# Attention with three softmaxes per head: two heads' global keys as one 128-column weight tile, value products issued in pairs of key rows, ten probability buffers

## What is computed

```python
attn = q @ k.T * scale                      # 16 heads of 8 channels
local_out  = softmax(where(|i - j| <= 128, attn, -inf)) @ v
topk_out   = softmax(q @ k[top 128 rows].T * scale) @ v[top 128 rows]
global_out = softmax(q @ k[first 64 rows].T * scale) @ v[first 64 rows]
out = (local_out + topk_out + global_out) / 3
```

## Time and profile before

| | us |
|---|---|
| median of 3 runs | 555.68 (554.42 to 555.85) |
| profiled execution | 551.48, span 549.6 |
| granted TensorE clock, mean | 0.993 |
| PE busy | 491.7 (89%) |
| DVE busy | 390.3 (71%) |
| ACT busy | 355.1 (65%) |
| POOL busy | 311.8 (57%) |

### The profile page before, as it was taken

The page is one execution under the profiler, slowest core; times in us unless marked ns, Lnnn a source line. Parts: engine busy times, 40 slices in busy tenths (PEclk is TensorE's granted clock), DMA queues, the critical chain, the costliest instruction groups (busy, mean ns, idle before and its releaser), DMA issues.

```text
span 549.6 us, 13411 instructions
## 1 busy us (share of the span) xinstructions
PE 491.7 (89%) x4427; PEld 305.4 (56%) x4427; DVE 390.3 (71%) x1400; ACT 355.1 (65%) x835; POOL 311.8 (57%) x464
## 2 busy tenths in 40 slices
PE   6999899889768899899789998999998999889996
PEld 3577677667334355345355454545554553577874
DVE  4877876469986698898877789677797893145325
ACT  7588565788008666657656857766665657657753
POOL 3411065457599975655059976689708336354540
PEclk9999999999889999999999999999999999999999
DMA  7999011765300000000000000001000101775606
GB/s 217 350 337 306 8 44 49 248 213 185 89 7 15 4 14 14 5 13 14 11 8 12 11 8 13 14 28 29 20 13 4 36 25 57 245 232 172 202 15 192
DMA packets 46006, 47.81 MB, mean 87 GB/s; under 512 B 8788, under 2 KB 37594, under 8 KB 45937
## 3 DMA queue, kind: packets, MB, share of 16 engines
q1 hardware_dynamic: 42928, 41.37, 24.3%
q0 software_dynamic: 3008, 5.58, 3.2%
HBM read 11.32 MB, written 19.48 MB: 56 GB/s over the span
## 4 chain that ended last, share of the span: by engine, by line
PE 63%; DVE 19%; issue 8%; ACT 6%; DMA 2%; POOL 1%; SPq 0%; DVEq 0%; ACTq 0%; POOLq 0%
PE BANK L1912 6%; PE BANK L1809 6%; PE BANK L1857 4%; PE BANK L1999 4%; PE BANK L1887 4%; PE BANK L1765 3%; PE BANK L1915 3%; PE BANK L1777 3%; PE BANK L1918 3%; DVE SW L1392 2%; DVE M L1390 2%; DVE QST L1438 2%; PE BANK L1792 2%; PE BANK L1882 2%; PE BANK L1862 2%
## 5 line engine op out<-in xcount | busy, mean ns | idle before, releaser
L1090 ACT ACTIVATE PT<-BANK 128x256 f32<-128x256 f32 (+2 forms) x352 | 161.9, 487 | 98.1 <-PE BANK L1887 71.2
L698 POOL TENSOR_SCALAR OH<-IOTA,POS 128x128 bf16<-128x128 bf16 x240 | 140.4, 605 | 4.7 <-DVE OH L1553 3.4
L1433 DVE CUSTOM_DVE_ANT_0 XN_a<-BANK,BANDQ 128x256 f32<-128x256 f32 (+1 forms) x128 | 62.3, 487 | 29.4 <-PE BANK L1857 25.6
L1433 DVE CUSTOM_DVE_ANT_0 XN_c<-BANK,BANDQ 128x384 f32<-128x384 f32 (+1 forms) x128 | 62.4, 487 | 14.2 <-PE BANK L1857 13.1
L706 POOL TENSOR_TENSOR SUM<-NRM 128x128 f32<-128x128 f32 x16 | 7.3, 456 | 96.8 <-DVE NRM L1454 96.8
L1912 PE MATMUL BANK<-PT,V 128*32 128x256 f32 (+1 forms) x512 | 47.7, 444 | 9.0 <-ACT OS L1099 8.6
L1438 DVE TENSOR_REDUCE QST<-BANK 128x4 f16<-128x512 f32 x64 | 42.3, 690 | 9.9 <-PE BANK L1862 9.6
L730 POOL DMA_INDIRECT yt_late<-QKV,IDY_late x31 | 30.4, 980 | 27.4 <-DVE QKV L1311 22.7
L1809 PE MATMUL BANK<-XNT_ALL,W 128*128 128x512 f32 x96 | 45.3, 597 | 0.0
L907 ACT ACTIVATE PT<-BANK 128x512 f32<-128x512 f32 x48 | 27.8, 598 | 19.1 <-PE BANK L1809 18.8
L1882 PE MATMUL BANK<-BANDK,IDB 128*128 128x256 bf16 x128 | 35.2, 275 | 0.4 <-ACT PT L1090 0.3
(11 more groups left out here) (371 smaller groups left out, 1299.6 us busy)
## 6 DMA issues: line engine op xcount, KB each, us to landing
xs_late<-W SPq DMA_DIRECT2D x1, 6984.0 KB, 39.3
xs_early<-W SPq DMA_DIRECT2D x1, 4680.0 KB, 18.9
KZB<-W SPq DMA_DIRECT2D x16, 256.0 KB, 2.6
KZC<-W SPq DMA_DIRECT2D x15, 256.0 KB, 2.3
PT<-W SPq DMA_DIRECT2D x11, 256.0 KB, 2.4
QKV<-xs_late SPq DMA_DIRECT2D x31, 72.0 KB, 1.9
W<-w SPq DMA_DIRECT2D x2, 1024.0 KB, 8.8
QKV<-xs_early SPq DMA_DIRECT2D x23, 72.0 KB, 2.5
```

The costliest lines, as they stand in the source:

```text
L698: last = nc.gpsimd.tensor_scalar(OH[g % 2][:, i, t, :], IOTA[:, :], POS[:, t, c:c + 1], None, ALU.is_equal)
L1090: nc.scalar.activation(PT[u % PT_RING][:, 0:w], P2_BANK[u % SCORE_RING][:, 0:w], ACT.Exp, scale=SCALE).then_inc(S["exp_done"], 1)
L1433: nc.vector.tensor_tensor_reduce(out=JUNK[v % 2][:, 0:n], in0=P1_BANK[v % SCORE_RING][:, 0:n], in1=BANDQ[:, off:off + n], scale=1.0, scala ...
```

## The change

1. Global keys. The second head's 64 global keys go into the first head's key tile, beside that head's own: columns 512 to 639 of the even tile hold two heads, in different partitions, and the top keys move to columns 640 to 767 in all tiles. The global p2 is one matmul with a 128-column weight tile instead of two of 64 columns; the global p1 is four matmuls of 128 columns instead of eight of 64, and the order in the bank changes accordingly, which the maximum reads in another order. `spread` issues six DMAs per group instead of four.
2. Value products. Rows 0 and 1 are issued together at u = 9, rows 2 and 3 at u = 17, rows T and T + 1 at u = 1 of the next group.
3. `PT` has ten buffers instead of eight.

```diff
--- before.py
+++ after.py
@@ -37,6 +37,8 @@
 SCALE = float(1.0 / (DH ** 0.5))
 KW = L + N_GLOBAL + K_TOP
 KG0, KS0 = L, L + N_GLOBAL
+PAIR_KEYS, TOP_KEYS = slice(L, L + 2 * N_GLOBAL), slice(L + 2 * N_GLOBAL, L + 2 * N_GLOBAL + K_TOP)
+SPREADS = HG + HG // 2
 TAKEN = -3.0e38
 OFF = -1.0e30
 SHIFT = 24
@@ -51,7 +53,8 @@
 ROWS = T + 2
 LEAD = 8
 FIRST_LEAD = 4
-PT_RING = 8
+PT_RING = 10
+PV_AT = {9: (0, 1), 17: (2, 3)}
 SCORE_RING = 3
 PART = DH + 1
 NG = B * GROUPS
@@ -434,6 +437,10 @@
 
         def spread_done(g):
 
+            return 16 * SPREADS * (g // 2 + 1)
+
+        def top_spread_done(g):
+
             return 16 * HG * (g // 2 + 1)
 
         def full(*use):
@@ -527,10 +534,20 @@
                              ).then_inc(R[w.tag]["zeroed"], 16)
 
 
-            def spread(g, lo, hi, done):
+            def spread(g):
+
+                for i in range(HG):
+                    r, a = slice(32 * i, 32 * i + 32), i % 2
+                    last = L if a else KS0
+                    sp.dma_start(KZ[g % 3][i][r, 0:last], KALL[g % 2][r, 0:last]).then_inc(KEYS_IN[g % 2], 16)
+                    if a:
+                        sp.dma_start(KZ[g % 3][i - 1][r, KG0 + N_GLOBAL:KG0 + 2 * N_GLOBAL], KALL[g % 2][r, KG0:KS0]
+                                     ).then_inc(KEYS_IN[g % 2], 16)
+
+            def spread_top(g):
                 for i in range(HG):
                     r = slice(32 * i, 32 * i + 32)
-                    sp.dma_start(KZ[g % 3][i][r, lo:hi], KALL[g % 2][r, lo:hi]).then_inc(done, 16)
+                    sp.dma_start(KZ[g % 3][i][r, TOP_KEYS], KALL[g % 2][r, KS0:KW]).then_inc(TOP_KEYS_IN[g % 2], 16)
 
             def tile_numbers(w, n):
 
@@ -576,18 +593,18 @@
             sp.wait_ge(S["misc_free"], free("qk", 0) + 1)
 
             sp.wait_ge(S["heads_zero"], 3)
-            spread(0, 0, KS0, KEYS_IN[0])
+            spread(0)
             results(EARLY)
             sp.wait_ge(S["misc_free"], free("qk", 1) + 1)
-            spread(1, 0, KS0, KEYS_IN[1])
+            spread(1)
             for g in range(NG):
 
 
                 if g >= 2:
                     sp.wait_ge(S["misc_free"], free("qk", g) + 1)
-                    spread(g, 0, KS0, KEYS_IN[g % 2])
+                    spread(g)
                 sp.wait_ge(S["misc_free"], free("kv", g) + 1)
-                spread(g, KS0, KW, TOP_KEYS_IN[g % 2])
+                spread_top(g)
 
             sp.wait_ge(R["late"]["table"], 1)
             sp.wait_ge(R["late"]["scattered"], 16 * 2 * LATE.jt)
@@ -1411,7 +1428,7 @@
                 dve.wait_ge(S["misc_full"], full("kv", g))
                 if g >= 2:
 
-                    dve.wait_ge(TOP_KEYS_IN[g % 2], spread_done(g - 2))
+                    dve.wait_ge(TOP_KEYS_IN[g % 2], top_spread_done(g - 2))
                 nc.vector.tensor_scalar(KALL[g % 2][:, KS0:KW], MISC[:, 0:K_TOP], KSH[:, TOP:TOP + 1], None, ALU.add)
                 nc.vector.reduce_sum(VSEL[g % 3][:, :, PART:PART + DH],
                                      MISC[:, K_TOP:K_TOP + HG * 3 * DH].rearrange("p (i s d) -> p i d s", i=HG, s=3),
@@ -1439,7 +1456,7 @@
                                          AX_X).then_inc(S["max_done"], 1)
                 else:
                     nc.vector.reduce_max(qst[:, :, h:h + GPAIR, SHIFT + GLOBAL],
-                                         P1_BANK[v % SCORE_RING][:, :].rearrange("p (a t s) -> p t a s", a=GPAIR, t=T),
+                                         P1_BANK[v % SCORE_RING][:, :].rearrange("p (t a s) -> p t a s", a=GPAIR, t=T),
                                          AX_X).then_inc(S["max_done"], 1)
 
             def divide(g):
@@ -1857,15 +1874,13 @@
                     last = mm(bank[:, 0:(hi - lo) * P], q[:, t * P:(t + 1) * P], k[:, lo * P:hi * P], start=True, stop=True)
                 elif t == T:
                     if w == TOP_W:
-                        pe.wait_ge(TOP_KEYS_IN[g % 2], spread_done(g))
+                        pe.wait_ge(TOP_KEYS_IN[g % 2], top_spread_done(g))
                     for s in range(T):
-                        last = mm(bank[:, s * K_TOP:(s + 1) * K_TOP], q[:, s * P:(s + 1) * P], k[:, KS0:KW], start=True, stop=True)
+                        last = mm(bank[:, s * K_TOP:(s + 1) * K_TOP], q[:, s * P:(s + 1) * P], k[:, TOP_KEYS], start=True, stop=True)
                 else:
                     for s in range(T):
-                        for a in range(GPAIR):
-                            lo = (a * T + s) * N_GLOBAL
-                            last = mm(bank[:, lo:lo + N_GLOBAL], q[:, s * P:(s + 1) * P], KZ[g % 3][i + a][:, KG0:KS0],
-                                      start=True, stop=True)
+                        last = mm(bank[:, s * GPAIR * N_GLOBAL:(s + 1) * GPAIR * N_GLOBAL], q[:, s * P:(s + 1) * P], k[:, PAIR_KEYS],
+                                  start=True, stop=True)
                 last.then_inc(S["p1_done"], 1)
 
             def p2(g, r, n):
@@ -1887,11 +1902,9 @@
                     last = mm(bank[:, 0:(hi - lo) * P], KZ[g % 3][n][:, r * P:(r + 1) * P], QT2[g % 2][:, lo * P:hi * P],
                               start=False, stop=True, skip_group_check=True)
                 elif r == T:
-                    last = mm(bank[:, :], KZ[g % 3][n][:, KS0:KW], QT2[g % 2][:, :], start=True, stop=True)
+                    last = mm(bank[:, :], KZ[g % 3][n][:, TOP_KEYS], QT2[g % 2][:, :], start=True, stop=True)
                 else:
-                    for a in range(2):
-                        last = mm(bank[64 * a:64 * a + 64, :], KZ[g % 3][2 * n + a][:, KG0:KS0], QT2[g % 2][:, :],
-                                  start=True, stop=True)
+                    last = mm(bank[:, :], KZ[g % 3][GPAIR * n][:, PAIR_KEYS], QT2[g % 2][:, :], start=True, stop=True)
                 last.then_inc(S["p2_done"], 1)
 
             def pv(g, r):
@@ -2068,9 +2081,10 @@
                     p2(g, r, n)
                     for v in scored_beside(g, u):
                         p1(*divmod(v, UNITS_Q))
-                    if n == 1 and r:
-                        pv(g, r - 1)
-                    elif n == 1 and g:
+                    for row in PV_AT.get(u, ()):
+                        pv(g, row)
+                    if u == 1 and g:
+                        pv(g - 1, T)
                         pv(g - 1, T + 1)
                     if u == qk_at(g) and g + 2 < NG:
                         transpose_qk(g + 2)
...
+            pv(NG - 1, T)
             pv(NG - 1, T + 1)
```

## The result

The changed kernel takes 566.48 us (median of 4 runs, 565.38 to 567.12), the kernel before in the same comparison 555.05. The ratio is 1.0226, with a 95% interval of 1.0197 to 1.0254: slower, by 10.9 to 14.1 us of 555. The forecast was 566.5.

A forecast was written before the change was run, and what follows sets the result against it. PE sets the pace, with ACT or DVE right behind in every stretch but A. Group sums of 12.7 us, taken as 11, on the profiled 551.48 give 562.5; 4.2 to the median makes 566.5, own range 560 to 572, overall 546 to 574.

The forecast's parts named there:

- A: Group 10 from unit 0 to unit 2: 2.15 us plus the top row's product, 0.98, gives 3.1 us.
- B: Group 10, unit 2 to the value product's end at u = 9: stays 5.6 us, ACT's queue still setting it.
- C: Group 10, from there to unit 18: 6.96 to 7.7 us, row 2's product, 0.78, no longer under DVE's work.
- D: Group 10, unit 18 to the next unit 0: 3.19 to 2.6 us, PE waiting nearly 1 us for QT2.
- The sum over the groups: All groups: +1.2 us for each of groups 7 to 13, 8.4 together; with the rest 12.7, of which 11 taken.
- a pair's own saving: On PE, a value product directly following another saves 0.12 us, three times a group: 0.36 us.
- the projection, 0.65 us, takes the place of the row 0 product under ACT's queue: Early groups, projection at u = 6: about -0.6 us in B, leaving +0.4 a group, 1.6 for groups 1 to 4.
- The cut from 12.7 to 11: Whole kernel: 11 of 12.7 us taken, since a walk counts every wait and treats B and C as independent.
- What costs nothing: SP's two extra copies a group (1.2 us) and the ten buffers add no wait; the buffers belong to the pairs.
- That PE alone counts: Rival, all 16 groups: PE's 0.8 us a group is gained, -13 us, 543; needs D below 2.2, C below 7; chance 0.22.
- The cancelling rival: Rival: gains and waits cancel, 555.7 within 2 us; needs a C loss of about 0.4, not 0.8; chance 0.13.
- The largest one: Rival: waits add up further, groups 1 to 6 also lose 1.2 us each, +17 us, 573; chance 0.13.

The follow-up runs named there:

- e8_row0_at7: Changed kernel with no value products paired, row 0's product at u = 7, the others in their old places, ten buffers: 553.30 us, ratio 0.9999.
- e9_tile_os_first: e1_tile with ACT's copy of the output bank behind exponential 2, ahead of the key copies, instead of behind exponential 3: ratio 0.9914, on another chip.
- e7_pair01: Changed kernel with only rows 0 and 1 still paired, the other value products in their old places: 551.96 us, ratio 0.9969.
- e5_row2_early: Changed kernel with row 2's product back at u = 13, the other pairs kept: 561.29 us, ratio 1.0161.
- e6_again19: Changed kernel with the second query transpose at u = 19 instead of 20: 563.85 us, ratio 1.0202.
- e2_pairs: Kernel before with the new order of value products and ten buffers, without the new global key tile: 566.08 us, ratio 1.0228.
- e3_ring8: Changed kernel with eight probability buffers instead of ten: 578.10 us, ratio 1.0450.
- e1_tile: Changed kernel with the old order of value products and eight buffers, so only the new global key tile: 551.39 us, ratio 0.9943.

## Why the prediction was right

**What bounds the kernel.** Right in that each stretch is set by the engine that was named for it, and that the new waits are larger than what PE saves: in group 10 PE's idle time went from 1.06 to 2.07 us. One sign did not come: PE's busy time was to fall by 13 us and fell by 3.1. The traces do not say how much of the rest is the lower clock (0.983 for 0.993) and how much the way through the array that the last matmul ahead of each new wait shows as busy. What PE saves is read from the distances between starts, below.

**A, forecast 3.1 us.** 3.01. The second of two products starts 0.88 us behind the first (376.19 to 377.07), not 0.98 as in the last group before.

**B, forecast 5.6, "not gained, only named differently".** 5.42, against 5.51 before by instruction starts. The tile alone, with the old order, has 5.49. `e8_row0_at7` and `e9_tile_os_first` put the product or the copy in two other orders and have 5.47 and 5.41, and `e7_pair01`, with this pair alone, has 5.42. What it is below the forecast is the pair again: 640 columns take 1.21 us where the step had 1.3 to 1.4.

**C, forecast 7.7.** 7.58. DVE's first top maximum starts 1.19 us behind the start of C, and the step in the shared bank 5.45 us behind it, forecast 1.17 and 5.41. Row 2's product is owed behind it. Only the place of the wait was told wrong: not p1's of units 14 to 16 wait in this group, but the gathering ahead of them, for DVE's division. Over the run p1's wait for top maxima 5.2 us, 4.6 before. `e5_row2_early` brings C back to 6.94.

**D, forecast 2.6.** 2.54, set by QT2: `e6_again19` makes it 2.05, and `e2_pairs` has the same 2.54 with 0.45 us more of work. The Trainium skill's page "TensorEngine Tiling (Array Packing)", section "PSUM Bottleneck", says that tiling speeds up TensorE but not the emptying of PSUM. The trace agrees: ACT, which empties the banks, is busy for 2.48 of D's 2.54 us.

**The sum over the groups** is where it was right by luck. That the median met the forecast to 0.02 us says little: the walk was to give 562.5 us for the profiled execution, and that took 566.20. The traces are 14.8 us apart for the forecast's 11, and the 3.8 missing were made up by the distance from the profiled execution to the median, taken as 4.2 us and 0.3 in the changed kernel.

Now the 14.8 us, group by group. An ordinary group was forecast at +1.2 and group 10 measured +0.74 by instruction starts (17.81 to 18.55); groups 7 to 13 came to 5.2 us instead of 8.4. What was mis-sized is a pair's own saving, 0.12 us each in the sum and some 0.25 measured: a lone product of rows 0 and 1 cost 0.10 + 0.57 and 0.10 + 0.78, 1.55, and the pair 0.10 + 1.21. Three pairs a group make about 0.4 us.

The other side was too low. The step that failed is "the projection, 0.65 us, takes the place of the row 0 product under ACT's queue, and I get about -0.6 for B" in groups 1 to 4. B stayed 6.16 us. PE's timeline of group 3 in the changed kernel shows why:

```profile
237.24 0.91 PE L1731 MATMUL BANK<-WQKV,XNT_ALL 128*128 128x384 f32 x2 [0.46 <-ACT KALL L953]
```

The projection writes the shared bank and waits until ACT has copied the last keys out of it; before, OS had hidden that wait. Groups 1 to 3 lost 1.0 to 1.1 us each instead of 0.4.

Group 4 lost 2.4, of which 1.5 are not in the forecast at all. Windows of the changed kernel there:

```profile
264.00:266.00 2.00, 1.36 (x37) 1.03 (x37) 1.97 (x4) 0.70 (x4) 1.50 (x4) 1.00 0.00 0
266.00:268.00 2.00, 0.86 (x3) 0.21 (x3) 1.97 (x7) 0.85 (x2) 1.89 (x2) 1.00 0.01 4
268.00:270.00 2.00, 1.58 (x7) 1.00 (x6) 1.97 (x7) 0.00 (x0) 0.00 (x0) 0.57 0.05 12
270.00:272.00 2.00, 2.00 (x17) 0.60 (x16) 0.50 (x4) 1.08 (x2) 0.00 (x0) 0.58 0.05 9
```

PE waits for DVE's top maxima without row 2's product to do, and the pair runs at half the clock: C of group 4 is 10.60 us, and 9.08 in `e2_pairs`, whose clock held. That the missing product is the cause isn't shown: `e5_row2_early` has it back in its place, and C there is still 9.40 us for the 8.43 of before, with the clock down to 0.50. Up to unit 0 of group 1 the forecast had -0.7 us and +1.7 were measured, 1.3 of them ahead of group 0; the kernels of the study differ by up to 3.6 us at that point (187.3 to 190.9 us on the first chip) without a relation to their order, so I put that down to no step. Groups 5 and 6 with 1.3 and group 14 with 0.2 are near their 1.4 and 0.5, and group 15 with what follows is 0.8 instead of 1.5. The cut from 12.7 to 11 was made for double counting, for which no run shows anything; the ordinary groups needed 3.2 for another reason, mostly the pair's own saving, and the early groups made up for it and more.

**What costs nothing.** No row of PE waits for a key copy. The ten buffers were told right, as `e3_ring8` shows. That DVE's other order of reading costs nothing is seen in its maxima of the global scores: 693 ns each before and in `e1_tile`, 694 in the changed kernel.

**Rivals.** That PE alone counts needed D below 2.2 and C below 7 and has neither. The cancelling rival needed a C loss of 0.4 and has 0.6. The largest one holds in a part: groups 1 to 4 do lose as much as the others.

## What to carry to other kernels

Work that stands between two waits on the leading engine is cover, even when it looks like an interruption. Before it is gathered elsewhere, look at what the following instruction waits for, and when that would be there without the work: row 2's product hid DVE's maxima and the top row's hid a copy. A saving that belongs to the leading engine alone (a tile filled twice, a mode entered once) is worth its price only in stretches where that engine is the last to be ready, and two edits that each shorten the same stretch do not add up. When a wait is attributed to one item of another engine's queue, moving that item or its reader can change the name of the wait and not its end, as long as the queue ahead of that end is as long. That is B here; in D, where the copy of QT2 was moved ahead of an exponential, the queue ahead of it did become shorter, and the stretch with it, by 0.48 us.

## What was not expected of the hardware

- Two column-tiled products back to back cost less than two apart by some 0.25 us, not by the 0.10 of entry: 1.21 us for 256 and 384 columns, against 0.57 and 0.78 and an entry each.
- Taking one 0.57 us product out of a stretch in which PE waits can cost the clock. In group 5 it is 1.00 throughout in all five kernels with the product at u = 5; in eight of nine without it B is 1.5 to 2.7 us longer, in `e7_pair01` with over 3 us at the lower level. The ninth kept its clock with as little to do.
- With two buffers too few, the writer's wait grew to 4.5 us at most and 66.7 in all, with 12 us of it in the time.
